# A two-layer GRU kernel: the n sums transposed into PSUM, the scan's result moved to another bank

## The chip, the cores and the metric

The kernel runs on 1 core of a Trainium2 chip. The metric is the device time of one execution in microseconds; the median of 3 runs before the change is 2195.38 us (2190.18 to 2202.85).

## The reference

Input `x` is (2, 1024, 256), with a condition vector (2, 256). First comes a conditioned GRU with a residual, then a mixture of experts with a residual:

```
ctx   = context[:, None, :]
mixed = tanh(x @ W_in.T + b_in + ctx)
h1 = gru(mixed, Wih0, Whh0, ...);  h2 = gru(h1, Wih1, Whh1, ...)
    # each of 1024 steps:  r = sigmoid(xr + hr); z = sigmoid(xz + hz)
    #                      n = tanh(xn + r * hn); h = (1 - z) * n + z * h
gate = sigmoid(context @ W_gate.T + b_gate)
x = x + (gate * h2 + h2) @ W_out.T + b_out
x = x + (shared(x) + routed(x)) / 3      # SwiGLU, and 2 of 8 GELU experts for each token
```

Everything is fp32, with batch 2 and hidden size 256. Two chains of 1024 dependent steps, one for each layer, run through the whole kernel.

## The kernel before, in words

**Slots.** The program is one long list of slots s = 0, 1, ... on every engine. Slot s holds step s of layer 0 and step s - 19 of layer 1 (LAG = 19), so that there are 1043 slots with GRU work. Into the slots the instructions of the mixture (L272 on TensorE, L745, L717, L721 and others on VectorE, L725 and others on ScalarE) are placed by a small planner, before or behind the work of a layer. Steps go in chunks of 16; two chunks have their own columns of a PSUM bank (p = 0, 1), and while one chunk runs, the next one's input projection (L306) is placed. j is the step's place in its chunk.

**One step of a layer.** TensorE adds the recurrent sums: in most steps first the r columns (L325, into bank l), then n and z (L333, into bank 2 + l). At two places of 16 in each layer (`r_first` is false) there is one wider group L333 with all three. VectorE turns 32x32 blocks so that the two batch rows come to lie in the free dimension: r (L395, to `r_pre`), n (L404, to `n_first`), z (L405, to `z_pre`), 64 elements in each partition. ScalarE makes the tanh of r (L466) into `n_second`. A scan on VectorE (L413, `dve_n`) joins `n_first` and `n_second` to the argument of n's tanh; its 12 results go to PSUM (`n_scan`). ScalarE makes the tanh of z (L472) and of n (L476) and a second scan (L424, `dve_h`) gives the new state, which TensorE loads as weights for the next step.

**Layout.** `n_first` and `n_second` are (128, ROWS, UB, 3): the transpose L404 writes element 2 of each triple, so that consecutive elements of its output lie 6 floats apart. Elements 0 and 1 of `n_first` are constants, set once at the start (L904, L905). `r_pre` and `z_pre` are (128, ROWS, UB), 2 floats apart. In PSUM, banks 0 and 1 hold the r sums of the layers (`r_sums`, 128 of 512 columns), banks 2 and 3 the other sums, banks 4 to 6 serve the mixture, and bank 7 holds `n_scan` of both layers.

**Once per chunk.** When the next chunk's projection is placed (`project_at`), `take_r` (L376) copies its r columns from bank 2 + l to bank l, and `take_n` (L380) transposes its n part to `n_second`. Layer 0 does both behind `dve_n` in slots with j = 13; layer 1 does `take_r` behind `dve_n` in slots with j = 1 and `take_n` in those with j = 2.

**Order on VectorE.** Each engine goes through its list in order, with waits on semaphores. In a slot VectorE has: r of layer 0, the state scan of layer 1 (previous step), n and z of layer 0, the n scan of layer 0, mixture work, the state scan of layer 0, then r, n, z and the n scan of layer 1, and mixture work.

Of the kernel before, what the change touches and what calls it, by code (L numbers as in the profile page):

```python
# [10 lines left out]
P = 128  # L11
B, T, D = 2, 1024, 256
KT = D // P
NQ = 4
U = D // NQ
UB = U // 32
NGATE = 4
CH = 16
ROWS = CH * B
# [21 lines left out]
def r_first(l, t):  # L41

    s = t + LAG * l
    return s % CH not in ((0, 4, 8, 12) if s >= SHORT else (4, 12))
# [74 lines left out]
def gru_moe_kernel(nc, a, out):  # L121
    with ExitStack() as ctx:
        def sb(name, *shape):
            return ctx.enter_context(nc.sbuf_tensor(name, list(shape), F32))
# [37 lines left out]
        stage = [sb(f"stage{l}", P, KT, ROWS) for l in range(2)]  # L162
        cells = [sb(f"cells{l}", P, CH * STEP) for l in range(2)]
        factors = [sb(f"factors{l}", P, STEP) for l in range(2)]
        n_first = [sb(f"n_first{l}", P, ROWS, UB, 3) for l in range(2)]
        r_pre = [sb(f"r_pre{l}", P, ROWS, UB) for l in range(2)]
        z_pre = [sb(f"z_pre{l}", P, ROWS, UB) for l in range(2)]
        n_second = [[sb(f"n_second{l}_{p}", P, ROWS, UB, 3) for p in range(2)] for l in range(2)]
# [26 lines left out]
        banks = [ctx.enter_context(nc.psum_tensor(f"bank{i}", [P, 512], F32)) for i in range(8)]  # L195
# [1 line left out]
        sums = [[banks[2 + l][:, p * NGATE * U:(p + 1) * NGATE * U] for p in range(2)] for l in range(2)]  # L197
        acc = banks[4][:, :].rearrange("p (m n) -> p m n", m=KT)
        ups = [banks[5 + i][:, :].rearrange("p (m n) -> p m n", n=TG) for i in range(2)]
        n_scan = [banks[7][:, 3 * B * UB * l:3 * B * UB * (l + 1)] for l in range(2)]  # L200

        s_ld = sem("s_ld")
        s_xld = [sem(f"s_xld{i}") for i in range(B * T // TB)]
# [35 lines left out]
        def own_rows(j):  # L239
            return slice(B * j, B * j + B)  # L240
# [21 lines left out]
        def schedule(s0, n):  # L262

            for s in range(s0, s0 + n):
                yield s, (s if s < T else None), (s - LAG if 0 <= s - LAG < T else None)
# [105 lines left out]
        def blocks(ap):  # L371
            return ap.rearrange("p (b i) -> p b i", i=32)

        def take_r(v, l, p):

            v.tensor_copy(r_sums[l][p], sums[l][p][:, 2 * U:3 * U])  # L376

        def take_n(v, l, p):

            v.transpose(n_second[l][p][:, :, :, 2].rearrange("p i b -> p b i"),  # L380
                        blocks(sums[l][p][:, 3 * U:])).then_inc(sets[l][1 - p]["xn"], 1)

        def dve_turn_r(v, l, t):

            p, j = t // CH % 2, t % CH
            s = sets[l][p]
            if r_first(l, t):
                v.wait_ge(s["r"], sum(r_first(l, i) for i in range(t - j, t + 1)))
                at = r_sums[l][p]
            else:  # L390
                v.wait_ge(s["pe"], j + 1)
                at = sums[l][p][:, 2 * U:3 * U]
            if j == CH - 1 and t < T - 1:
                v.wait_ge(s["go"], 1)
            v.transpose(r_pre[l][:].rearrange("p i b -> p b i"), blocks(at)).then_inc(s["turn"], 1)  # L395

        def dve_turn_nz(v, l, t):

            p, j = t // CH % 2, t % CH
            s = sets[l][p]  # L400
            v.wait_ge(s["pe"], j + 1)
            if j == 0:
                v.wait_ge(sets[l][1 - p]["xn"], 1)
            v.transpose(n_first[l][:, :, :, 2].rearrange("p i b -> p b i"), blocks(sums[l][p][:, 0:U])).then_inc(s["for_n"], 1)  # L404
            v.transpose(z_pre[l][:].rearrange("p i b -> p b i"), blocks(sums[l][p][:, U:2 * U])).then_inc(s["turn"], 1)  # L405

        def dve_n(v, l, t):

            p, j = t // CH % 2, t % CH
            s = sets[l][p]  # L410
            own = own_rows(j)
            v.wait_ge(s["for_n"], 2 * (j + 1))
            v.tensor_tensor_scan(n_scan[l], n_first[l][:, own].rearrange("p i b e -> p (i b e)"),  # L413
                                 n_second[l][p][:, own].rearrange("p i b e -> p (i b e)"), 0.0, ALU.mult, ALU.add)\
                .then_inc(s["n"], 1)

        def dve_h(v, l, t):

            p, j = t // CH % 2, t % CH
            s = sets[l][p]  # L420
            v.wait_ge(s["for_h"], 2 * (j + 1))
            if j == CH // 2:
                v.wait_ge(s["pool"], 1)
            v.tensor_tensor_scan(step_cells(l, (j + 1) % CH, 0), factors[l][:, 2:], step_cells(l, j), 0.0, ALU.mult, ALU.add)\  # L424
                .then_inc(s["h"], 1)

        def dve_slots(v, s0, n, base):
            for s, t0, t1 in schedule(s0, n):
                c, j = divmod(s, CH)
                p = c % 2  # L430
                if t0 is not None and r_first(0, t0):
                    dve_turn_r(v, 0, t0)
                if 0 <= s - 1 - LAG < T:
                    dve_h(v, 1, s - 1 - LAG)
                if t0 is not None and not r_first(0, t0):
                    dve_turn_r(v, 0, t0)
                if t0 is not None:
                    dve_turn_nz(v, 0, t0)
                    dve_n(v, 0, t0)
                    if j == 13 and t0 < T - CH:  # L440
                        v.wait_ge(sets[0][p]["x"], 1)
                        take_r(v, 0, 1 - p)
                        take_n(v, 0, 1 - p)
                mixture_at(v, "dve", s, 0, base)
                if t0 is not None:
                    dve_h(v, 0, t0)
                if t1 is not None:
                    dve_turn_r(v, 1, t1)
                    dve_turn_nz(v, 1, t1)
                    dve_n(v, 1, t1)  # L450
                if CH <= s < T + CH and j == 1:
                    v.wait_ge(sets[1][p]["x"], 1)
                    take_r(v, 1, 1 - p)
                if CH <= s < T + CH and j == 2:
                    take_n(v, 1, 1 - p)
                mixture_at(v, "dve", s, 1, base)
# [175 lines left out]
        def mixture_at(eng, engine, s, part, base):  # L632

            mix = in_window(s)
            if mix is None:
                return
            h = (s - mix.begin) * 2 + part
            for at, name, waits, issue in mix.ops[engine]:
                if at != h:
                    continue  # L640
                for w in waits:
                    wait_for(eng, mix, w)
                half = h // mix.window
                if name == "out00" and mix is mixtures[0]:
                    eng.wait_ge(s_mld, 16 * len(late_loads))
                    eng.wait_ge(s_mix, B * NTB * KT)
                if name == "out00" and mix is not mixtures[0]:
                    eng.wait_ge(m_sets[1]["dve"], before(mix).value[before(mix).y_done])
                if name == "out00":
                    eng.wait_ge(sets[1][mix.end // CH % 2]["pool"] if mix is not mixtures[-1] else s_hist, 2)  # L650
                if mix.value[name] == mix.total(engine, half) and not (mix is mixtures[-1] and half == 1):
                    eng.wait_ge(m_sets[half]["go"], 1)
                issue(eng, mix.first * B).then_inc(m_sets[half][engine], 1)
# [245 lines left out]
        def _(v):  # L899
# [31 lines left out]
            take_r(v, 0, 0)  # L931
            take_n(v, 0, 0)
            run(v, dve_slots)

        @block.scalar
# [77 lines left out]
```

## Time and profile before

| | us |
|---|---|
| median of 3 runs | 2195.38 |
| span of the profiled execution | 2185.8 |
| TensorE matmul busy | 2068.4 (95%) |
| VectorE busy | 1841.5 (84%) |
| ScalarE busy | 1201.4 (55%) |
| GpSimd busy | 560.5 (26%) |

The span goes from the first to the last instruction of one profiled execution; the page gives no other time for that execution. The mean granted TensorE clock is 0.998 of full speed. Busy TensorE is not TensorE at its peak, since matmuls overlap and their ends are modelled. The page's chain that ended last is 60% TensorE, 26% VectorE and 10% ScalarE. Instructions of one engine overlap as well: the next one can start before the one ahead has ended, so that on VectorE the distance from start to start says more than a duration.

### The profile page before, as it was taken

The page shows a single profiled execution, that of the slowest core. Times are in us where ns is not written, and L with a number is a line of the kernel's source. Part 1 is how long each engine was busy: PE and PEld are TensorE (multiplying, and loading weights), DVE is VectorE, ACT ScalarE, POOL GpSimd, SP SyncE. Part 2 cuts the span into 40 slices and gives each one's busy share as a digit, 9 for nine tenths or more (in the row PEclk, how much of TensorE's full clock was granted, in tenths as well). Part 3 has the DMA queues.
Part 4 walks back from the last instruction along what each step waited for, and adds up shares of the span by engine and source line. Part 5 has one row for each costly group of instructions (what it writes and reads, how often), then busy time and mean ns, then how long its engine had stood idle before and what let it go on. Part 6 is the DMA issues. An engine that isn't in the chain of part 4 may idle for free.

```text
span 2185.8 us, 162058 instructions
## 1 busy us (share of the span) xinstructions
PE 2068.4 (95%) x69920; PEld 1485.0 (68%) x69920; DVE 1841.5 (84%) x11225; ACT 1201.4 (55%) x6471; POOL 560.5 (26%) x2542
## 2 busy tenths in 40 slices
PE   6989899999999999999999999999999999999987
PEld 3666666677666776767767676666767676777766
DVE  4888889888888888888888888888888888888874
ACT  2555555555555555555555555555555555555542
POOL 1222232222322223222222222222232222222220
PEclk9999999999999999999999999999999999999999
DMA  5000000000000000000000000000000000000000
GB/s 219 4 4 5 4 5 5 24 5 5 9 5 24 5 5 10 5 24 5 10 5 24 5 5 9 5 24 5 5 10 5 24 5 10 5 21 9 5 16 19
DMA packets 10879, 32.76 MB, mean 15 GB/s; under 512 B 1368, under 2 KB 6832, under 8 KB 9136
## 3 DMA queue, kind: packets, MB, share of 16 engines
q1 hardware_dynamic: 10160, 22.38, 2.8%
q8 instruction: 548, 8.98, 1.7%
q14 instruction: 171, 1.40, 0.2%
HBM read 20.22 MB, written 2.16 MB: 10 GB/s over the span
## 4 chain that ended last, share of the span: by engine, by line
PE 60%; DVE 26%; ACT 10%; issue 3%; DMA 1%; SPq 0%; POOL 0%; DVEq 0%; POOLq 0%
PE bank L333 29%; PE bank L325 17%; PE bank L272 11%; DVE n_first L404 9%; DVE cells L424 7%; ACT factors L472 6%; ACT cells L476 4%; DVE r_pre L395 4%; DVE z_pre L405 3%; PE bank L306 3%; DVE bank L413 1%; DVE n_second L380 0%; DVE x L687 0%; PE bank L657 0%; DVE hid L745 0%
## 5 line engine op out<-in xcount | busy, mean ns | idle before, releaser
L333 PE MATMUL bank<-w_h,cells 128*22 128x128 f32 (+4 forms) x32768 | 1363.4, 281 | 23.6 <-DVE cells L424 13.9
L333 PEld LDWEIGHTS bank<-w_h,cells 128*22 128x22 f32 (+4 forms) x32768 | 853.0, 111 | 130.5 <-DVE cells L424 91.3
L325 PEld LDWEIGHTS bank<-w_h,cells 128*2 128x2 f32 (+15 forms) x28112 | 512.2, 113 | 528.1 <-DVE cells L424 502.8
L517 POOL TENSOR_SCALAR cells<-cells 128x4 f32<-128x4 f32 x2048 | 463.6, 226 | 1525.8 <-DVE cells L424 1524.8
L325 PE MATMUL bank<-w_h,cells 128*2 128x64 f32 (+15 forms) x28112 | 770.1, 225 | 76.3 <-DVE cells L424 55.5
L466 ACT ACTIVATE n_second<-r_pre 128x4 f32<-128x4 f32 x2048 | 426.3, 208 | 508.8 <-DVE r_pre L395 466.3
L472 ACT ACTIVATE factors<-z_pre 128x4 f32<-128x4 f32 x2048 | 429.6, 210 | 436.5 <-DVE z_pre L405 358.8
L404 DVE STREAM_TRANSPOSE n_first<-bank 128x64 f32<-128x64 f32 x2048 | 600.0, 293 | 33.1 <-PE bank L333 23.7
L424 DVE TENSOR_TENSOR_SCAN cells<-factors,cells 128x18 f32<-128x18 f32 x2048 | 397.2, 194 | 241.5 <-ACT cells L476 177.1
L395 DVE STREAM_TRANSPOSE r_pre<-bank 128x64 f32<-128x64 f32 x2048 | 480.6, 235 | 33.3 <-PE bank L325 24.9
L405 DVE STREAM_TRANSPOSE z_pre<-bank 128x64 f32<-128x64 f32 x2048 | 427.4, 209 | 0.0
L413 DVE TENSOR_TENSOR_SCAN bank<-n_first,n_second 128x12 f32<-128x12 f32 x2048 | 396.7, 194 | 5.3 <-ACT n_second L466 1.1
L476 ACT ACTIVATE cells<-bank 128x8 f32<-128x8 f32 x2048 | 367.6, 180 | 1.4 <-DVE bank L413 0.2
L272 PE MATMUL bank<-x,w_1e 128*32 128x256 f32 (+3 forms) x2304 | 162.3, 357 | 2.3 <-issue 2.3
L272 PE MATMUL bank<-hid,w_2e 128*32 128x256 f32 (+3 forms) x2304 | 157.6, 356 | 1.8 <-DVE hid L745 1.8
L306 PE MATMUL bank<-w_x,stage 128*32 128x192 f32 x2048 | 131.9, 327 | 1.6 <-DVE z_pre L405 0.9
L272 PE MATMUL bank<-x,w 128*32 128x256 f32 (+3 forms) x1152 | 81.9, 356 | 0.2 <-DVE hid L721 0.2
L272 PEld LDWEIGHTS bank<-x,w_1e 128*32 128x32 f32 x2304 | 73.2, 110 | 2.6 <-issue 0.3
L272 PEld LDWEIGHTS bank<-hid,w_2e 128*32 128x32 f32 x2304 | 70.2, 110 | 5.4 <-DVE hid L745 2.4
L306 PEld LDWEIGHTS bank<-w_x,stage 128*32 128x32 f32 x2048 | 63.9, 109 | 14.2 <-DVE z_pre L405 1.4
L745 DVE TENSOR_TENSOR hid<-act_t,c_all 128x128 f32<-128x128 f32 (+2 forms) x240 | 66.4, 277 | 1.2 <-issue 0.7
L478 ACT ACTIVATE bank<-biases 128x256 f32<-128x256 f32 x124 | 47.5, 383 | 0.0
(91 smaller groups left out, 558.8 us busy)
## 6 DMA issues: line engine op xcount, KB each, us to landing
c_all<-weights SPq DMA_DIRECT2D x6, 1024.0 KB
x_t<-in_x_t SPq DMA_DIRECT2D x4, 512.0 KB, 7.4
w_1e<-in_w_1e SPq DMA_DIRECT2D x1, 2048.0 KB
w_2e<-in_w_2e SPq DMA_DIRECT2D x1, 2048.0 KB
w_x<-in_w_x SPq DMA_DIRECT2D x2, 768.0 KB, 8.2
w_h<-in_w_h SPq DMA_DIRECT2D x2, 768.0 KB, 9.5
w<-in_w SPq DMA_DIRECT2D x3, 512.0 KB
out_y<-y SPq DMA_DIRECT2D x6, 256.0 KB, 3.5
```

The costliest lines, as they stand in the source:

```text
L272: mm = pe.matmul(ps[strip], w[:, strip], x, start=start, stop=stop, tile_position=(0, 32 * g), skip_group_check=True)
L325: mm = pe.matmul(r_sums[l][p][32 * g:32 * g + B * (j + 1)], state_tile(l, j, kt), w_h[l][:, kt, g, 2 * U:], start=False, stop=False, tile_ ...
L333: mm = pe.matmul(sums[l][p][32 * g:32 * g + B * (j + 1), 0:width], state_tile(l, j, kt), w_h[l][:, kt, g, 0:width], start=False, stop=Fals ...
L395: v.transpose(r_pre[l][:].rearrange("p i b -> p b i"), blocks(at)).then_inc(s["turn"], 1)
L404: v.transpose(n_first[l][:, :, :, 2].rearrange("p i b -> p b i"), blocks(sums[l][p][:, 0:U])).then_inc(s["for_n"], 1)
L405: v.transpose(z_pre[l][:].rearrange("p i b -> p b i"), blocks(sums[l][p][:, U:2 * U])).then_inc(s["turn"], 1)
L413: v.tensor_tensor_scan(n_scan[l], n_first[l][:, own].rearrange("p i b e -> p (i b e)"), n_second[l][p][:, own].rearrange("p i b e -> p (i ...
L424: v.tensor_tensor_scan(step_cells(l, (j + 1) % CH, 0), factors[l][:, 2:], step_cells(l, j), 0.0, ALU.mult, ALU.add)\
L466: act.activation(n_second[l][p][:, own, :, 0], r_pre[l][:, own], ACT.Tanh, scale=0.5).then_inc(s["for_n"], 1)
L472: act.activation(cell_part(factors[l][:], 2), z_pre[l][:, own_rows(j)], ACT.Tanh, scale=0.5)
L476: act.activation(to, n.to_broadcast([P, B, UB, 2]), ACT.Tanh).then_inc(s["for_h"], 1)
L517: pool.tensor_scalar(cell_part(step_rows(l, j), 3), cell_part(step_rows(l, j), 1), 0.5, None, ALU.mult)\
```

## The change

`n_first` moves from SBUF to PSUM bank 7, the columns of layer l from 192 l on, in the same layout. `n_scan`, the result of the n scan, moves from bank 7 to columns 128 to 139 of bank l, behind the r sums of that layer. `take_r`, which writes bank l, is placed ahead of `dve_n` instead of behind it, for both layers, and for layer 0 the wait for the projection goes with it. `take_n` stays behind `dve_n`. No instruction is added or taken away.

```diff
-        n_first = [sb(f"n_first{l}", P, ROWS, UB, 3) for l in range(2)]
...
-        n_scan = [banks[7][:, 3 * B * UB * l:3 * B * UB * (l + 1)] for l in range(2)]
+        n_scan = [banks[l][:, 2 * U:2 * U + 3 * B * UB] for l in range(2)]
+        n_first = [banks[7][:, 3 * ROWS * UB * l:3 * ROWS * UB * (l + 1)].rearrange("p (r b e) -> p r b e", b=UB, e=3) for l in range(2)]
...
                     dve_turn_nz(v, 0, t0)
-                    dve_n(v, 0, t0)
                     if j == 13 and t0 < T - CH:
                         v.wait_ge(sets[0][p]["x"], 1)
                         take_r(v, 0, 1 - p)
+                    dve_n(v, 0, t0)
+                    if j == 13 and t0 < T - CH:
                         take_n(v, 0, 1 - p)
...
                     dve_turn_nz(v, 1, t1)
-                    dve_n(v, 1, t1)
                 if CH <= s < T + CH and j == 1:
                     v.wait_ge(sets[1][p]["x"], 1)
                     take_r(v, 1, 1 - p)
+                if t1 is not None:
+                    dve_n(v, 1, t1)
                 if CH <= s < T + CH and j == 2:
                     take_n(v, 1, 1 - p)
```

## Rows read from the trace of the kernel before

**Rows 1.** Timeline, one slot: start us, us, engine, line, operation, output<-inputs, count
```profile
1007.20 0.20 DVE L424 TENSOR_TENSOR_SCAN cells<-factors,cells 128x18 f32<-128x18 f32 x1 [0.24 <-ACT cells L476]
...
1007.70 0.62 PE L333 MATMUL bank<-w_h,cells 128*16 128x128 f32 x16
...
1008.28 0.20 DVE L424 TENSOR_TENSOR_SCAN cells<-factors,cells 128x18 f32<-128x18 f32 x1
1008.39 0.29 DVE L404 STREAM_TRANSPOSE n_first<-bank 128x64 f32<-128x64 f32 x1
...
1008.56 0.21 DVE L405 STREAM_TRANSPOSE z_pre<-bank 128x64 f32<-128x64 f32 x1
...
1008.72 0.19 DVE L413 TENSOR_TENSOR_SCAN bank<-n_first,n_second 128x12 f32<-128x12 f32 x1
...
1009.16 0.20 DVE L424 TENSOR_TENSOR_SCAN cells<-factors,cells 128x18 f32<-128x18 f32 x1 [0.25 <-ACT cells L476]
```

**Rows 2.** Chain of waits in order of time, same slot: start us, us, what
```profile
1007.45 0.43 PE bank L325 x16
1007.88 0.44 PE bank L333 x16
1008.32 0.43 PE bank L272 x8
1008.75 0.22 PE bank L325 x16
```

**Rows 3.** Waits: who for whom, us in total, times, longest
```profile
PEld bank L325 <- DVE cells L424: 502.8, 1601, 1.4
```

**Rows 4.** Groups by shape, VectorE: count, busy us, mean ns, idle before
```profile
L404 DVE STREAM_TRANSPOSE n_first<-bank 128x64 f32<-128x64 f32 x2048 | 600.0, 293 | 33.1 <-PE bank L333 23.7
L395 DVE STREAM_TRANSPOSE r_pre<-bank 128x64 f32<-128x64 f32 x2048 | 480.6, 235 | 33.3 <-PE bank L325 24.9 <-PE bank L333 6.6
L405 DVE STREAM_TRANSPOSE z_pre<-bank 128x64 f32<-128x64 f32 x2048 | 427.4, 209 | 0.0
L424 DVE TENSOR_TENSOR_SCAN cells<-factors,cells 128x18 f32<-128x18 f32 x2048 | 397.2, 194 | 241.5 <-ACT cells L476 177.1
L413 DVE TENSOR_TENSOR_SCAN bank<-n_first,n_second 128x12 f32<-128x12 f32 x2048 | 396.7, 194 | 5.3 <-ACT n_second L466 1.1
L745 DVE TENSOR_TENSOR hid<-act_t,c_all 128x128 f32<-128x128 f32 x192 | 53.1, 277 | 0.5 <-issue 0.5
...
L376 DVE COPY bank<-bank 128x64 f32<-128x64 f32 x128 | 27.3, 214 | 0.2 <-PE bank L306 0.2
L721 DVE SCALAR_TENSOR_TENSOR hid<-mid,bank 128x128 f32<-128x128 f32 x52 | 14.4, 277 | 0.7 <-PE bank L272 0.3 <-issue 0.2
```

**Rows 5.** Groups by shape, ScalarE
```profile
L714 ACT ACTIVATE act_t<-bank 128x256 f32<-128x256 f32 x24 | 9.1, 378 | 0.0
...
L693 ACT ACTIVATE score_th<-bank,r_bias 8x128 f32<-8x128 f32 x12 | 4.2, 354 | 0.0
...
L714 ACT ACTIVATE act_t<-bank 128x128 f32<-128x128 f32 x4 | 1.1, 277 | 3.0 <-PE bank L272 2.0 <-DVE top L768 1.0
...
L693 ACT ACTIVATE score_th<-bank,r_bias 8x64 f32<-8x64 f32 x2 | 0.5, 305 | 5.1 <-PE bank L272 5.1
```

**Rows 6.** Timeline, a step of layer 0 in which r is not first
```profile
1002.49 0.26 DVE L404 STREAM_TRANSPOSE n_first<-bank 128x64 f32<-128x64 f32 x1
...
1002.60 0.21 ACT L466 ACTIVATE n_second<-r_pre 128x4 f32<-128x4 f32 x1 [0.40 <-DVE r_pre L395]
1002.62 0.21 DVE L405 STREAM_TRANSPOSE z_pre<-bank 128x64 f32<-128x64 f32 x1
1002.84 0.19 DVE L413 TENSOR_TENSOR_SCAN bank<-n_first,n_second 128x12 f32<-128x12 f32 x1
```

**Rows 7.** Timeline, a slot with take_r (L376)
```profile
997.89 0.21 DVE L376 COPY bank<-bank 128x64 f32<-128x64 f32 x1
...
998.01 0.24 DVE L395 STREAM_TRANSPOSE r_pre<-bank 128x64 f32<-128x64 f32 x1
```

## The prediction, made before the changed kernel ran

> **What bounds the kernel now.** I read the timeline first, because the page's shares average over two recurrences that share every engine, then the chain of waits in order of time, then the waits, and last the groups by shape for the prices.
>
> In one undisturbed slot [rows 1] the reader is to see the loop that each layer runs through once per time step. From the state scan L424 at 1007.20 to the same scan at 1009.16 it is 1.96 us. Its pieces: 1.12 us from the scan's start until the z and n matmuls L333 have ended (1007.70 + 0.62 = 1008.32), 0.07 us until the n transpose L404 starts, 0.33 us until the n scan L413 starts (1008.39 to 1008.72), and 0.44 us for that scan, ScalarE's tanh and the hand back to L424 (1008.72 to 1009.16). The n scan starts 0.04 us after the end of L404 (1008.39 + 0.29 = 1008.68), so the transpose's whole duration lies in the loop. The other layer runs the same loop about half a slot apart: its L424 at 1008.28 stands directly ahead of L404, 0.11 us before it.
>
> The chain of waits [rows 2] is all TensorE there, which looks like a TensorE bound and isn't quite one. A first group of r matmuls takes 0.43 us after a wait and 0.22 us when it follows other matmuls, so 0.21 us of a slot is TensorE's own latency. What it must stream per slot is 2 x 0.22 + 2 x 0.44 + 0.43 = 1.75 us, and only where a block of the mixture (L272) stands in the slot. The waits [rows 3] say the same: weight loads of L325 waited 1601 times for the state scan, 0.31 us each. So the loops' latency binds, with TensorE 0.2 us behind it. There are 1024 + 19 = 1043 slots, and 2185.8 / 1043 = 2.10 us on average: slots with projections or fuller queues are longer than this one.
>
> **The change part by part.**
>
> *n_first into bank 7.* This touches the write of L404 and one input of L413. All three transposes read 64 elements of PSUM, and yet L404 takes 293 ns, L405 209 and L395 235 [rows 4]. What differs is where elements land: r_pre and z_pre are written at a step of 8 bytes, n_first at 24 bytes (6 floats). The layout therefore costs some 60 to 84 ns in SBUF. No row shows VectorE writing PSUM at a step, so I bound it: below, the transpose falls to the 209 to 235 ns of its neighbours (a copy from PSUM to PSUM of the same 64 elements took 214, so writing PSUM itself costs nothing); above, it keeps its 293 ns, and as far as rows go it could also double its excess to about 375. The nearest row for PSUM at a step is ScalarE's read of every other float, L693 [rows 5]: from 64 to 128 elements it grows by (354 - 305) / 64 = 0.77 ns an element, and the dense read of L714 by (378 - 277) / 128 = 0.79. A step in PSUM costs that engine nothing, one element at a time. VectorE is slower than that anyway: (277 - 209) / 64 = 1.06 ns an element between L405 and L745 [rows 4]. I take 225 ns.
>
> The Trainium skill speaks against it (PSUM — Partial Sum Buffer, Specifications): PSUM has 8-byte lines and "any non-contiguous AP slows matmuls significantly", while the skill's page SBUF — State Buffer (Specifications) gives SBUF 16-byte lines of which each needs two hits for full speed. By the second, the excess in SBUF is explained, and the trace agrees: a step of 8 bytes costs nothing and one of 24 does. By the first, a 24-byte step would cost in PSUM as well; then nothing is won here. That is a rival below; the row of L693 shows a read and another engine, not this write.
>
> With the write at full speed the n scan can't start at the end of L404 + 0.04 = 0.26 us only; it also stands in VectorE's queue behind L405. Unhindered, one transpose starts 0.13 us after another (L404 1002.49, L405 1002.62 [rows 6]), so the scan comes at 0.13 + 0.13 = 0.26 us, against 0.33: 0.07 us less in each loop.
>
> *Reading it back.* L413 now takes one input from PSUM, the other stays in SBUF. L721 reads one of each and took 277 ns for 128 elements, L745 with both in SBUF 277 [rows 4]. I take 0; the ends are 0 and +65 ns.
>
> The Trainium skill has a price for this (VectorE: DVE Perf Modes, "The TRN2 errata"): 58 cycles fixed for an operation from SBUF and 120 from PSUM. Worked out from that page it would be an estimate of 62 / 0.96 = 65 ns more per scan, and the whole gain would go. The two rows above disagree with it.
>
> *The scan's result in bank l instead of bank 7.* L413 already writes PSUM, 194 ns for 12 elements, like L424's 194 for 18 in SBUF [rows 4]; only the bank changes, price 0. TensorE's next r sums of that layer go to this bank after L424, so after ScalarE has read the result: no new wait. Both ends are near 0, since the accesses to the bank are in order already.
>
> *take_r ahead of the scan* (and its wait with it). Once per 16 steps and layer, 63 + 64 = 127 times. The wait is for a projection that TensorE issued ahead of the matmuls that L404 has already waited for, so it is met. Before, the copy L376 stood behind the n scan in the 0.44 us that VectorE waits for ScalarE: covered. Now it stands between L405 and L413, and the next instruction follows a copy after 0.12 us (997.89 to 998.01 [rows 7]). Behind it wait the scan, the tanh, the state scan and so the next step. Cost 127 x 0.12 = 15 us, the ends 8 (the two layers' delays overlap) and 15. take_n stays behind the scan, covered as before.
>
> **Does 0.07 us reach the end?** Each loop contains one such interval, and so does a loop through both layers (L424 of one, L404 of the other, its state scan, TensorE's queue), so the slot shortens by 0.07 where latency binds: 1.96 to 1.89, still above 1.75. Not so in the 2 of 16 steps of each layer where r isn't computed first: there the scan waits for ScalarE (L466 ends at 1002.60 + 0.21 = 1002.81, the scan starts at 1002.84 [rows 6]), and L404 isn't its limit. These are 4 of 16 slots, and in each the other layer may keep its gain; I count 13 of 16: 1043 x 13/16 x 0.07 = 59 us. Less 15: a gain of 44 to 45 us. What is late next is L405's place in the queue, then ScalarE's L466, then TensorE's stream.
>
> The span of the profiled execution, 2185.8 us, becomes 2141. The page gives no own time for that execution beyond its span; the median shown, 2195.38, is 9.6 us more, for what lies around it, and the change leaves that alone. Forecast 2150 us. Its own range: 14 of 16 slots, 0.08 us and 8 us for the copies give 2195 - 73 + 8 = 2130; 12 of 16 and 0.05 us give 2195 - 39 + 15 = 2171.
>
> **Rivals.**
>
> 1. *The step costs in PSUM too* (slower). Place: the write of L404. If it still takes 293 ns or more, the 0.33 us stays and the 15 us for the copies come on top: 2210 us. It decides from the point where L404 in PSUM takes some 275 ns: 0.02 us x 850 slots just pays for the copies. For it: every element lands on an address of its own, 24 bytes on. Against: rows 5. Were the excess doubled, 0.08 x 850 more, 2278.
> 2. *The scan pays for a PSUM input*: 0.065 us on L413 takes the 0.07 back, 2207 us. For it only a rule; against it L721 and L745.
> 3. *TensorE becomes the bound.* If in slots with projections and mixture blocks the stream is late, the gain holds in half of the slots: 1043 / 2 x 0.07 = 37, less 15, 2173 us. For it: the chain of waits shows TensorE unbroken, and the average slot is 2.10, not 1.96. Against: 1601 waits for the state scan.
> 4. *The copies are hidden again*, for instance because the other layer has slack there: 2195 - 59 = 2136 us, inside my range.
>
> **How the numbers follow.** Forecast with 4: 0.56. Rival 3: 0.12. Rival 1: 0.18, most of it near 2210, a part with an excess between (2185 to 2205). Rival 2: 0.14, of which half lands between, since a smaller price than 65 ns is as likely. I call no change what is within 0.5% (11 us). Faster: 0.56 + 0.12 and little of the in-between cases, 0.68. Same 0.13. Slower 0.19. The range of 8 in 10: 2122 (0.08 us in nearly all slots, copies partly hidden) to 2212, which takes in the plain form of rivals 1 and 2 and leaves their heavier forms out.
>
> **What would show it.** L404 at 210 to 235 ns instead of 293, and L405 starting 0.13 us behind it; L413 still near 194; start of L404 to start of L413 0.26; the undisturbed slot 1.89 us; L376 directly ahead of L413, its scan 0.12 us later than in other slots. L404 at 290 or more, or L413 at 250, would make the prediction wrong; L404 short and the slot still 1.96 would mean that TensorE's stream binds.

## The result, and the profile after

The changed kernel takes 2181.28 us (median of 6 runs, 2178.72 to 2187.65) against 2194.0 us for the kernel before (6 runs). The ratio is 0.9944, 95% interval 0.9923 to 0.9964: 12 us faster where 45 were forecast. The profiled execution has a span of 2176.9 us and a time of 2178.72, against a span of 2185.8 before. The ratios leave out a few much longer executions, most of them at a lower granted clock. The line numbers on ScalarE are 2 higher than before (L466 is now L468, L476 is L478).

The groups by shape on VectorE, changed kernel (count, busy us, mean ns, idle before):

```profile
L404 DVE STREAM_TRANSPOSE bank<-bank 128x64 f32<-128x64 f32 x2048 | 520.4, 254 | 58.9 <-PE bank L333 36.8
L395 DVE STREAM_TRANSPOSE r_pre<-bank 128x64 f32<-128x64 f32 x2048 | 480.1, 234 | 36.8 <-PE bank L325 26.3 <-PE bank L333 7.3
L405 DVE STREAM_TRANSPOSE z_pre<-bank 128x64 f32<-128x64 f32 x2048 | 427.8, 209 | 0.0
L424 DVE TENSOR_TENSOR_SCAN cells<-factors,cells 128x18 f32<-128x18 f32 x2048 | 396.3, 193 | 249.5 <-ACT cells L478 179.0
L413 DVE TENSOR_TENSOR_SCAN bank<-bank,n_second 128x12 f32<-128x12 f32 x2048 | 380.2, 186 | 5.0 <-ACT n_second L468 1.1
```

They answer to [rows 4]. L404 writes PSUM now and takes 254 ns on average instead of 293; 225 were forecast. The average mixes situations, told apart by when L405 follows: where that is under 0.14 us later, L404 takes 221 ns (262 before), and where it is 0.17 us later, 265 (305 before). So the write is 41 ns quicker in both, and the forecast fits the first. The n scan L413 reads one input from PSUM and is no slower but faster, 186 instead of 194. r and z are as they were.

The timeline of two neighbouring steps in the changed kernel, which answers to [rows 1]:

```profile
1002.53 0.20 DVE L424 TENSOR_TENSOR_SCAN cells<-factors,cells 128x18 f32<-128x18 f32 x1
1002.64 0.25 DVE L404 STREAM_TRANSPOSE bank<-bank 128x64 f32<-128x64 f32 x1
...
1002.80 0.21 DVE L405 STREAM_TRANSPOSE z_pre<-bank 128x64 f32<-128x64 f32 x1
...
1002.93 0.18 DVE L413 TENSOR_TENSOR_SCAN bank<-bank,n_second 128x12 f32<-128x12 f32 x1
...
1003.15 0.18 ACT L478 ACTIVATE cells<-bank 128x8 f32<-128x8 f32 x1
1003.36 0.20 DVE L424 TENSOR_TENSOR_SCAN cells<-factors,cells 128x18 f32<-128x18 f32 x1 [0.24 <-ACT cells L478]
...
1003.72 0.27 DVE L404 STREAM_TRANSPOSE bank<-bank 128x64 f32<-128x64 f32 x1
...
1003.89 0.21 DVE L405 STREAM_TRANSPOSE z_pre<-bank 128x64 f32<-128x64 f32 x1
1004.02 0.18 DVE L413 TENSOR_TENSOR_SCAN bank<-bank,n_second 128x12 f32<-128x12 f32 x1
...
1004.25 0.18 ACT L478 ACTIVATE cells<-bank 128x8 f32<-128x8 f32 x1
...
1004.46 0.19 DVE L424 TENSOR_TENSOR_SCAN cells<-factors,cells 128x18 f32<-128x18 f32 x1
```

From the start of L404 to the start of L413 it is 0.29 us in the first step (1002.64 to 1002.93) and 0.30 in the second (1003.72 to 1004.02). It was 0.33, and 0.26 were forecast. Over the whole trace the mean is 0.311 us where no take_r stands between, against 0.338 before, and from L413 to the next L424 it is 0.435 against 0.442. From the state scan at 1002.53 to that at 1004.46 it is 1.93 us, where 1.96 were before and 1.89 forecast. If every one of the 1043 slots had gained these 0.03 us, 31 us would be gone from the time, before anything is paid for take_r.

The slot with take_r, changed kernel, answers to [rows 7]:

```profile
1028.03 0.27 DVE L404 STREAM_TRANSPOSE bank<-bank 128x64 f32<-128x64 f32 x1
1028.20 0.21 DVE L405 STREAM_TRANSPOSE z_pre<-bank 128x64 f32<-128x64 f32 x1
1028.33 0.20 DVE L376 COPY bank<-bank 128x64 f32<-128x64 f32 x1
1028.44 0.18 DVE L413 TENSOR_TENSOR_SCAN bank<-bank,n_second 128x12 f32<-128x12 f32 x1
```

L376 stands between L405 and L413 as forecast, and the scan comes 0.11 us after it: 0.41 us after L404.

The waits tell where the rest went. Columns: who for whom, us in total, times, longest; "issue" means that the engine waited for nothing that the profile shows.

```profile
PEld bank L325 <- DVE cells L424: 465.6, 1522, 1.3
...
PEld bank L333 <- issue: 23.9, 61, 1.4
...
PEld bank L325 <- issue: 11.6, 21, 3.2
...
PEld bank L272 <- issue: 6.8, 22, 0.7
...
PEld bank L306 <- issue: 0.9, 2, 0.8
```

In the kernel before, the same four rows for the weight loads are:

```profile
PEld bank L333 <- issue: 13.6, 34, 1.3
PEld bank L325 <- issue: 9.7, 11, 2.7
...
PEld bank L272 <- issue: 3.3, 13, 0.5
...
PEld bank L306 <- issue: 0.9, 2, 0.7
```

The sum grew from 27.5 to 43.2 us. The state scan, for which the weight loads waited 502.8 us before [rows 3], is waited for 465.6 us now: the recurrences did get quicker, and TensorE makes up for a part of it by stopping on its own. One such stop, weight loads of the changed kernel, in the middle of a group of 16 for one step:

```profile
1007.53 0.28 PEld L325 LDWEIGHTS bank<-w_h,cells 128*18 128x18 f32 x16 [0.25 <-DVE cells L424]
1007.73 0.28 PEld L333 LDWEIGHTS bank<-w_h,cells 128*18 128x18 f32 x9
1008.56 0.15 PEld L333 LDWEIGHTS bank<-w_h,cells 128*18 128x18 f32 x5 [0.56 <-issue]
```

Nine of sixteen loads go out, then there is nothing for 0.56 us, then the group goes on. No operand is missing, since the other seven need nothing that the first nine didn't need.

### The profile page after: what moved, and what is told of

The parts are those of the page before. It is cut to its first block, busy times and chain, and to the rows that moved or that the text cites. A ratio compares the mean times of both kernels' runs of the same rounds, so it can differ in the third digit from the quotient of the medians.

```text
span 2176.9 us, 162058 instructions
## 1 busy us (share of the span) xinstructions
PE 2059.9 (95%) x69920; PEld 1498.2 (69%) x69920; DVE 1794.4 (82%) x11225; ACT 1140.4 (52%) x6471; POOL 559.1 (26%) x2542
## 3 DMA queue, kind: packets, MB, share of 16 engines
q8 instruction: 547, 8.96, 1.7%
## 4 chain that ended last, share of the span: by engine, by line
PE 60%; DVE 25%; ACT 10%; issue 3%; DMA 1%; SPq 0%; POOL 0%; DVEq 0%; POOLq 0%
PE bank L333 28%; PE bank L325 18%; PE bank L272 11%; DVE bank L404 8%; DVE cells L424 7%; ACT factors L474 6%; DVE z_pre L405 5%; DVE r_pre L395 4%; ACT cells L478 4%; PE bank L306 2%; DVE bank L413 1%; DMA x_t<-in_x_t 0%; DVE x L689 0%; PE bank L659 0%; DVE hid L747 0%
## 5 line engine op out<-in xcount | busy, mean ns | idle before, releaser
L333 PEld LDWEIGHTS bank<-w_h,cells 128*22 128x22 f32 (+4 forms) x32768 | 862.1, 111 | 131.4 <-DVE cells L424 83.0
L325 PEld LDWEIGHTS bank<-w_h,cells 128*2 128x2 f32 (+15 forms) x28112 | 524.7, 113 | 499.6 <-DVE cells L424 465.6
L325 PE MATMUL bank<-w_h,cells 128*2 128x64 f32 (+15 forms) x28112 | 778.2, 225 | 75.2 <-DVE cells L424 55.9
L468 ACT ACTIVATE n_second<-r_pre 128x4 f32<-128x4 f32 x2048 | 426.2, 208 | 509.4 <-DVE r_pre L395 471.4
L424 DVE TENSOR_TENSOR_SCAN cells<-factors,cells 128x18 f32<-128x18 f32 x2048 | 396.3, 193 | 249.5 <-ACT cells L478 179.0
L404 DVE STREAM_TRANSPOSE bank<-bank 128x64 f32<-128x64 f32 x2048 | 520.4, 254 | 58.9 <-PE bank L333 36.8
L405 DVE STREAM_TRANSPOSE z_pre<-bank 128x64 f32<-128x64 f32 x2048 | 427.8, 209 | 0.0
L413 DVE TENSOR_TENSOR_SCAN bank<-bank,n_second 128x12 f32<-128x12 f32 x2048 | 380.2, 186 | 5.0 <-ACT n_second L468 1.1
L478 ACT ACTIVATE cells<-bank 128x8 f32<-128x8 f32 x2048 | 360.4, 176 | 0.4 <-DVE bank L413 0.2
```

Source lines behind the costliest of these rows:

```text
L325: mm = pe.matmul(r_sums[l][p][32 * g:32 * g + B * (j + 1)], state_tile(l, j, kt), w_h[l][:, kt, g, 2 * U:], start=False, stop=False, tile_ ...
L333: mm = pe.matmul(sums[l][p][32 * g:32 * g + B * (j + 1), 0:width], state_tile(l, j, kt), w_h[l][:, kt, g, 0:width], start=False, stop=Fals ...
L468: act.activation(n_second[l][p][:, own, :, 0], r_pre[l][:, own], ACT.Tanh, scale=0.5).then_inc(s["for_n"], 1)
L478: act.activation(to, n.to_broadcast([P, B, UB, 2]), ACT.Tanh).then_inc(s["for_h"], 1)
```

## What TensorE stops for

The page says what TensorE's instructions weigh:

```profile
PE 2059.9 (95%) x69920; PEld 1498.2 (69%) x69920; DVE 1794.4 (82%) x11225; ACT 1140.4 (52%) x6471; POOL 559.1 (26%) x2542
...
q8 instruction: 547, 8.96, 1.7%
```

139,840 matmuls and weight loads at 64 bytes would be 8.95 MB, and the queue named "instruction" brings 8.96 MB in 547 packets, so it is nearly all TensorE's code: one packet of 16 KB in 4.0 us. The 64 bytes come out of e9 below: with 9,504 TensorE instructions fewer, the queue brings 37 packets fewer, 606 KB. I took from the trace all places where a weight load starts over 200 ns after the start of the one ahead and doesn't follow the end of a state scan by less than 90 ns, between 30 and 2150 us of the span, and asked how long before the end of each the last packet of that queue had landed. This table is worked out from the records; it is no view of the profile. Its sums are distances from start to start, so that each holds the load ahead too, some 0.1 us.

```
kernel                            pauses   us in sum   ended 1.2 to 1.6 us after a packet
before                                71        37.5     59
layout alone (e6)                    127        65.0    110
changed                              117        58.6    101
before, few columns (e7)             106        55.6     87
layout alone, few columns (e8)       152        79.1    125
before, few strips (e9)               43        19.2     15
layout alone, few strips (e10)        74        32.8     35
changed, few strips (e14)             71        31.0     36
```

At random moments of the span about 10% fall into that window behind a packet; of the pauses 82 to 87% do in the kernels that issue all strips, and 35 to 51% in those with few, where a larger share must have another cause. That points to the code supply; the experiments below change how much code there is.

## The experiments

"Layout alone" is the changed kernel with take_r in its old place and n_scan behind n_first in bank 7. Ratios are to the kernel before on the same chip.

**e1: the order alone.** n_first and n_scan as before, only take_r moved:

```diff
                     dve_turn_nz(v, 0, t0)
-                    dve_n(v, 0, t0)
                     if j == 13 and t0 < T - CH:
                         v.wait_ge(sets[0][p]["x"], 1)
                         take_r(v, 0, 1 - p)
+                    dve_n(v, 0, t0)
+                    if j == 13 and t0 < T - CH:
                         take_n(v, 0, 1 - p)
```

(and the same for layer 1.) 

> The kernel before with only the order changed: take_r (L376) stands ahead of the n scan, n_first stays in SBUF, n_scan in bank 7. Theory A (what the prediction charged): 126 scans come 0.11 to 0.12 us later and each delay reaches the end: +14 us, ratio 1.006. Theory B (the other layer's slack hides it): under +4 us, ratio 1.000 to 1.002. In the trace both see start of L404 to start of L413 at 0.45 us in those slots; they differ in whether the next steps of the other layer start later.

Ratio 1.0014 (0.9996 to 1.0032): 3 us, near theory B. In this layout the scan had waited for the end of L404 anyway, so it comes only 0.08 us later in those slots (0.42 instead of 0.34 us after L404, on average over the trace). That would be 126 x 0.08 = 10 us if every delay reached the end.

**e3: order and bank of the result.**

```diff
-        n_scan = [banks[7][:, 3 * B * UB * l:3 * B * UB * (l + 1)] for l in range(2)]
+        n_scan = [banks[l][:, 2 * U:2 * U + 3 * B * UB] for l in range(2)]
```

> The kernel before with the order of take_r changed and n_scan moved to the r sums' bank; n_first stays in SBUF. It tells why L413 fell from 194 to 186 ns and L413 to L424 from 0.443 to 0.435 us. If that is the bank of the result: L413 at 186 here and a time 5 us below e1. If it is the input read from PSUM: L413 stays at 194 and the time is that of e1.

Ratio 1.0009 (0.9993 to 1.0025), L413 at 192 ns in e1 and in e3. The bank of the result makes no difference; what is left for the quicker scan of the changed kernel is its input in PSUM.

**e2 and e6: the layout alone**, run twice.

```diff
-        n_scan = [banks[l][:, 2 * U:2 * U + 3 * B * UB] for l in range(2)]
+        n_scan = [banks[7][:, 6 * ROWS * UB + 3 * B * UB * l:6 * ROWS * UB + 3 * B * UB * (l + 1)] for l in range(2)]
```

> The changed kernel with the order of before: n_first in bank 7, and n_scan in bank 7 too, behind it (columns 384 on), take_r behind the n scan. If the start of L404 to the start of L413 is 0.035 us shorter and L413 to L424 0.008 us shorter, as in the changed kernel, a latency bound (theory A) with 13 of 16 slots passing it on gives 1043 x 0.043 x 13/16 = 36 us less than before, ratio 0.983. Theory B: TensorE's queue takes half of it back (start of L404 later after the state scan), 18 to 25 us less, ratio 0.989 to 0.992. If reading and writing one bank slows the scan, L413 is over 200 ns and the ratio is near 1.

> The layout alone (order of take_r as before, n_scan behind n_first in bank 7) once more. Ratio to before 0.988 to 0.993, faster than the changed kernel by 3 to 14 us as the two theories of the kernel beside it say.

Ratios 0.9903 (0.9874 to 0.9932) and 0.9910 (0.9885 to 0.9934): 20 us, theory B's size, though its cause was named wrongly, as e7 and e8 show. Reading and writing one bank in one scan costs nothing (L413 at 187 ns).

**e5: the changed kernel again**, beside e6.

> The changed kernel once more, beside the next one on the same chip, to price the order of take_r in the new layout. Ratio to before 0.992 to 0.996. Theory A (each of the 126 delays of 0.11 us reaches the end): 14 us above the layout alone. Theory B (part is absorbed where the other layer or TensorE is late anyway): 3 to 9 us above it.

Ratio 0.9929 (0.9906 to 0.9952), in the medians 3 us above e6 (2180.49 and 2177.22). The intervals overlap: in the full kernel the price of the order can't be told within 0 to some 11 us.

**e4: L404 writes without a step.**

```diff
-            v.transpose(n_first[l][:, :, :, 2].rearrange("p i b -> p b i"), blocks(sums[l][p][:, 0:U])).then_inc(s["for_n"], 1)
+            v.transpose(n_dense[l], blocks(sums[l][p][:, 0:U])).then_inc(s["for_n"], 1)
```

> The changed kernel, but L404 writes its 64 results dense in bank 7 in columns that nothing reads, and the scan reads an element 2 that stays 0: the n sums are left out of the result, all instructions and waits stay. Theory A (the duration of L404 sets the scan's start): L404 falls from 254 to about 225 ns and the scan starts 0.03 us sooner, 20 to 25 us less than the changed kernel, ratio 0.983. Theory B (VectorE's queue sets it: L404 to L405 0.17 us, L405 to L413 0.13 us): L404 gets shorter, the start of L404 to the start of L413 stays 0.30 us, and the time is within 5 us of the changed kernel, ratio 0.993 to 0.996. If L404 stays at 254, no step in PSUM costs anything, and 254 is the price of writing PSUM with a transpose.

```profile
L405 DVE STREAM_TRANSPOSE bank<-bank 128x64 f32<-128x64 f32 x2048 | 520.9, 254 | 63.6 <-PE bank L334 41.3
...
L414 DVE TENSOR_TENSOR_SCAN bank<-bank,n_second 128x12 f32<-128x12 f32 x2048 | 380.7, 186 | 4.9 <-ACT n_second L469 1.1
```

L404 (here L405) takes 254 ns with a step of 24 bytes and 254 without. By situation it is the same: 222 and 265 ns, against 221 and 265. So a step in PSUM costs nothing. The 254 are again an average over these situations and no fixed price of a transpose into PSUM. Ratio 0.9941 (0.9919 to 0.9963), as the changed kernel. The third branch of the expectation held. Since L404 kept its length, this run can't tell the two conditions on the scan apart, the end of L404 and the place behind L405.

**e7 and e8: TensorE streams less.** Each mixture product computes 32 of 256 columns:

```diff
-            return lambda pe, col: by_columns(pe, ps, w, x, start, stop)
+            return lambda pe, col: by_columns(pe, ps[:, 0:32], w, x[:, 0:32], start, stop)
```

> The kernel before with TensorE relieved: every product of the mixture computes 32 of its 256 columns and leaves the other columns out; instructions and waits stay. It is the base for the next kernel. If the recurrences' latency alone set the slot, the time would be that of before less 2%; if TensorE's stream holds some slots, it is 60 us and more below before (2 to 6%).

> The layout alone with TensorE relieved in the same way (32 of the mixture's 256 columns, the others left out). Theory A (TensorE's stream took back the other half of the gain): the distance to the relieved kernel before grows from 21 us to 1043 x 0.043 x 14/16 = 39 us, 33 to 45. Theory B (something on VectorE or ScalarE takes it back, such as ScalarE's tanh of r or a state scan in front): the distance stays at 15 to 27 us.

Ratios 0.9994 (0.9976 to 1.0011) and 0.9915 (0.9889 to 0.9941). The distance is 17 us, theory B, and the relieved kernel isn't faster. One caution: the granted clock was 0.5 (1.2 GHz) from 2134 us on in e7, for 61 us, and from 2113 us on in e8, for 55. More than half of each stretch still has slots in it: the last 27 state scans took 55.0 and 52.9 us, against 46.7 and 45.9 in the kernel before and in e6. So 7 to 8 us of gain are hidden in each, and the distance between the two is hardly touched. What came in place of the stream is in the weight loads' waits of e7:

```profile
PEld bank L333 <- issue: 25.9, 63, 1.9
PEld bank L325 <- issue: 12.8, 17, 3.0
PEld bank L272 <- issue: 8.6, 26, 1.1
PEld bank L306 <- issue: 2.1, 6, 0.8
```

They come to 49.4 us where the kernel before has 27.5, with the same instructions; in e8 they come to 62.0 where e6 has 49.0. TensorE's streamed time was not what took half of the gain back.

**e9 and e10: TensorE gets fewer instructions.** One strip of four:

```diff
-            return lambda pe, col: by_columns(pe, ps, w, x, start, stop)
+            def one(pe, col):
+                return pe.matmul(ps[0:32], w[:, 0:32], x, start=start, stop=stop, tile_position=(0, 0), skip_group_check=True)
+            return one
```

> The kernel before, with only one of the four 32-column strips of every mixture product issued (three quarters of the mixture's outputs are left out; waits and signals stay). TensorE gets 7% fewer instructions, the streamed time per strip is the same. Theory C (TensorE waits for its own code: the long gaps in its weight loads end 1.2 to 1.6 us after a 16 KB code packet has landed): such gaps, 71 over 200 ns and 37 us in sum before, become fewer, and the time falls 15 to 35 us, ratio 0.984 to 0.993. Theory D (the gaps come from something else, such as the pairing of the two layers' queues): ratio within 0.003 of 1, as with 32 of 256 columns.

> The layout alone, with the same three quarters of the mixture's products left out. Theory C: the distance to the kernel before with the same left out grows from 20 us to 30 to 39 us, since the code now keeps up. Theory D: it stays at 15 to 24 us.

Ratios 0.9832 (0.9806 to 0.9858) and 0.9676 (0.9650 to 0.9701): 2161.2 and 2125.9 us. The kernel before becomes 36 us faster, and the distance grows from 20 to 35 us. That is theory C on both counts. It matters here that one strip holds TensorE nearly as long as four. In the chain of waits in order of time, e9:

```profile
1002.15 0.41 PE bank L659 x2
```

That is a product of one strip, and in [rows 2] the product of four strips takes 0.43 us. So e9 and e10 take out instructions and nearly no streamed time: at most 0.02 us for each of some 700 products, 14 us in all. The "issue" waits of the weight loads fall from 27.5 to 10.3 us in e9. That is 17 of the 36 us; the rest isn't located. The waits of e10's weight loads, in the same columns as above:

```profile
PEld bank L333 <- issue: 10.8, 25, 1.5
...
PEld bank L272 <- issue: 2.3, 10, 0.2
PEld bank L306 <- issue: 2.2, 4, 0.8
...
PEld bank L325 <- issue: 1.2, 2, 0.8
```

These come to 16.5 us, and 17.0 with one more of 0.5 at L660, the line of the single strips. The same rows of the layout alone with all strips (e6) come to 49.0:

```profile
PEld bank L333 <- issue: 29.2, 62, 2.0
...
PEld bank L325 <- issue: 11.5, 22, 2.8
...
PEld bank L272 <- issue: 7.2, 20, 0.9
...
PEld bank L306 <- issue: 1.1, 2, 0.7
```

**e14: the changed kernel with few strips.** The same edit.

> The changed kernel with one of four strips of each mixture product issued (three quarters of the mixture left out): the price of take_r ahead of the scan once the code keeps up. Theory A (all 126 delays of 0.11 us reach the end): 14 us above the layout alone with the same left out (2126), 2140 us. Theory B (the code stalls and the other layer's slack had absorbed it; only the slack remains here): 5 to 10 us above it, 2131 to 2136 us. If it is within 3 us the order costs nothing, even here.

Ratio 0.9732 (0.9717 to 0.9747) against 0.9676 for e10: 2138.0 us, 12 above e10 with an uncertainty of some 7, nearest to theory A. With the code waits mostly gone, take_r ahead of the scan costs what was forecast for it.

**e11, e12 and e13: fewer instructions, nothing left out.** Each product as matmuls of the full 128 columns of the array, one in place of four strips (e11 on the kernel before, e12 on the layout alone) or, by the same edit with a loop over two strips, as two strips of 64 (e13, layout alone):

```diff
-            return lambda pe, col: by_columns(pe, ps, w, x, start, stop)
+            return lambda pe, col: pe.matmul(ps, w, x, start=start, stop=stop, skip_group_check=True)
```

> The kernel before, with each mixture product as one 128-column matmul instead of four strips of 32 columns; nothing is left out. Theory C: TensorE has 7% fewer instructions to load, and if a full product streams as long as the four strips together, the time falls 15 to 35 us, ratio 0.984 to 0.993. Rival: passing from strips to the full array and back makes TensorE drain twice a product, some 0.1 us in each slot with mixture work, and the time rises 20 us and more.

> The layout alone with full-width mixture products: the candidate for a better kernel than both. Theory C: ratio 0.974 to 0.985, and the distance to the kernel before with full-width products is over 28 us. If the drain rival holds, it is above the layout alone (0.991).

> The layout alone with each mixture product as two strips of 64 columns instead of four of 32; nothing is left out, TensorE has 3% fewer instructions. If only the full array drains and half-width strips run among the 32-column ones, code supply wins: ratio 0.978 to 0.987, faster than the layout alone (0.991). If any change of strip width makes TensorE drain, as the full width did: ratio 1.02 to 1.03.

Ratios 1.0421 (1.0395 to 1.0446), 1.0298 (1.0272 to 1.0323) and 1.0204 (1.0187 to 1.0221): the size of the drain rival, each time. TensorE's matmuls in e11:

```profile
1010.23 0.42 PE L325 MATMUL bank<-w_h,cells 128*22 128x64 f32 x16
1010.46 0.62 PE L333 MATMUL bank<-w_h,cells 128*22 128x128 f32 x16
1011.01 0.70 PE L658 MATMUL bank<-hid,w_2e 128*128 128x256 f32 x2
1011.64 0.43 PE L325 MATMUL bank<-w_h,cells 128*16 128x64 f32 x16
```

The r matmuls of the next layer start 0.63 us after the full-width product (1011.01 to 1011.64), though their state was there; in [rows 2] a product of four strips holds TensorE for 0.43 us. Single records of the traces (medians) split this further. From the last matmul ahead to the product it is 0.20 us in e11 and 0.09 in the kernel before. From the first to the second matmul of the product, both full width, it is 0.32 us, and 0.22 between two single strips in e9. From the second to the next r matmul it is 0.31. So some 0.2 us lie at the two changes of width and 0.1 between two matmuls of one width.

The Trainium skill has a rule for the first part (TensorEngine Tiling (Array Packing), Key Properties): changing the tiling mode drains TensorE. The trace agrees with it for the 0.2 us; the 0.1 us between equal widths is no such change.

## Why the prediction was wrong

- *What bounds the kernel.* Right as to the two loops of 1.96 us. Incomplete: the waits of the kernel before have 27.5 us of "issue" at the weight loads, and the prediction has no term for them. It took the stream of 1.75 us per slot for the next limit; the runs point to TensorE's code.
- *n_first into bank 7: a step costs nothing in PSUM.* Right (e4). The Trainium skill's "any non-contiguous AP slows matmuls significantly" (PSUM — Partial Sum Buffer, Specifications) speaks of matmuls, and carrying it over to this VectorE write fails. The 225 ns were right for the steps in which L404 takes 221, and too short for the 242 to 265 of those that count. No run has a dense transpose into SBUF, so "a step of 8 bytes costs nothing" is not shown.
- *"Unhindered, one transpose starts 0.13 us after another."* This is the step that failed for the first half. The 0.13 was read in [rows 6], a step in which r is not first. In the whole trace before, L405 follows within 0.14 us in 336 of 2048 steps, and in these the n scan starts 0.35 us after L404, since it waits for ScalarE's tanh of r. The changed kernel has 319 such steps, and still 0.35 us:

```profile
1000.66 0.22 DVE L404 STREAM_TRANSPOSE bank<-bank 128x64 f32<-128x64 f32 x1
...
1000.77 0.21 ACT L468 ACTIVATE n_second<-r_pre 128x4 f32<-128x4 f32 x1 [0.41 <-DVE r_pre L395]
...
1000.79 0.21 DVE L405 STREAM_TRANSPOSE z_pre<-bank 128x64 f32<-128x64 f32 x1
1001.01 0.19 DVE L413 TENSOR_TENSOR_SCAN bank<-bank,n_second 128x12 f32<-128x12 f32 x1
```

  So the short distance comes just where it wins nothing. In the other steps L405 follows after 0.15 to 0.17 us, before [rows 1] as after. There 0.17 + 0.13 = 0.30, and the end of L404 + 0.04 is 0.30 too (0.28 by either where L405 follows after 0.15): both conditions on the scan come out at the same place, 0.03 to 0.04 us less than before, not 0.07.
- *Reading it back: 0.* Nearly right, 6 to 8 ns better. The Trainium skill's 62 more cycles for an operation from PSUM (VectorE: DVE Perf Modes, "The TRN2 errata") don't show in this scan, which has one input there.
- *Does 0.07 us reach the end, in 13 of 16 slots?* This failed for the second half. The layout alone has 28 ns less from L404 to the scan and 5 less behind it, which is 34 us in 1043 slots, and few-strip kernels show 35 +- 8; with all strips 20 arrive. The 14 or 15 us that are missing are covered by the weight loads' "issue" waits, 27.5 us before and 49.0 in e6. These are single traces: the old layout has 37.2 and 38.3 in e3 and e1, the new one 39.7 to 54.0 in five runs. In the few-strip pair the waits rise by 6.7 us only. My reading is that time spent waiting for the state scan, during which code could come in, was taken out, so that TensorE ran ahead of its code more often; the rise is shown, this reason for it is argued. Rival 3 had the engine right, and also that about half of the gain doesn't arrive; it named the stream as the cause, and e7 and e8 speak against that.
- *take_r: 15 us.* Right within the noise where there is less code (12 +- 7, e14); there are 126 such scans, not 127. In the full kernel it is 3 us by the medians beside each other, presumably since a delay there also gives the code time to arrive; that part is argued and not shown.
- *The sum.* Forecast -59 + 15. Shown: -35 + 12 = -23 without code waits, and -20 plus some 3 to 9 with them, measured -12 and, in e5, -16. The 2181 us lie inside the range of 2122 to 2212 because the range was wide enough for rivals that didn't come true.

Not settled: how far ahead TensorE's code is fetched, why a pause ends just 1.2 to 1.6 us after a packet has landed, and where the other 19 of e9's 36 us come from. Also, which of the two conditions holds the scan at 0.30 us was not tested, nor why L405 follows after 0.13 in some steps and 0.17 in others.

The better of the versions is the layout alone: 0.9903 and 0.9910, against 0.9944 and 0.9929 for the changed kernel. The scan's result needn't leave bank 7. VectorE touches that bank next at L404 of the other layer, which in its list stands behind the state scan, and the state scan waits for ScalarE to have read the result. So take_r can stay in the 0.44 us that are free. The step from one to the other is within the intervals' overlap; few-strip kernels show it clear of noise.

## What to carry to other kernels

Take the distance between two instructions from a place where they stand in the same situation, with the same wait just ended in front of them: the smallest distance in the trace belongs to another case. Where small instructions by the ten thousand keep an engine busy, set its code bytes and the "issue" waits beside the stream before counting on a shorter chain: here nearly half of what the chain gave didn't arrive, and the waits for code grew by about that much. And before paying for a new order to keep accesses to a bank apart, look whether the waits that exist keep them apart already.

## What the runs showed of the hardware that was not expected

- A VectorE transpose of 64 elements takes 254 ns on average into PSUM at a step of 24 bytes and 254 dense (e4); into SBUF 293 at that step. By situation, 221 or 265 ns into PSUM and 262 or 305 into SBUF.
- A scan with one input from PSUM takes 186 to 187 ns, with both from SBUF 192 to 194.
- 9,504 instructions fewer of 139,840 on TensorE (7%) made the kernel 36 us faster (e9); seven eighths fewer mixture columns in the same instructions made it 2 us faster, with some 8 more hidden by a granted clock of 0.5 at the end (e7).
- A mixture product of one 32-column strip holds TensorE for 0.41 us, one of four strips for 0.43.
- Passing from 32-column strips to 128-column matmuls and back costs more than it saves here: 2290 us against 2197 (e11).
